# A two-layer convolution kernel on one core: the upper half of x by a rounding DMA, the lower half and the chain steps at other places in the strip

## The chip, the cores and the metric

The kernel runs on one core of one Trainium2 chip. The metric is the device time of one execution in microseconds (us). The kernel before takes 3897.72 us, the median of three runs (3897.64 to 3898.21).

## The reference

The input x is 16 images of 128 channels by 128 by 128 pixels, float32. Two layers follow, each a residual around a group normalisation (32 groups of 4 channels):

```
# layer 0
g  = group_norm(x)
xh = w_in @ g + b_in                                # 1x1, 128 -> 256 channels
k  = relu(mean(xh) @ kg_w1.T + kg_b1) @ kg_w2.T + kg_b2   # a 3x3 kernel per image and channel
y  = depthwise_conv3x3(xh, k);  y = y * tanh(softplus(y))     # Mish
x  = x + w_out @ y + b_out                          # 1x1, 256 -> 128 channels
# layer 1
f  = fftshift(fft(group_norm(x), over channels)) * mask
x  = x + relu(real(ifft(ifftshift((amp_w @ f.real + amp_b) + i*(ph_w @ f.imag + ph_b)))))
```

The transforms run over channels only, so layer 1 is one 128 by 128 matrix on the channels of each pixel, which is built once (`lt`), scaled per image by the inverse root of the variance (`lpt`), and followed by the relu.

## The kernel before, in words

An image is cut into 16 strips of 8 rows (1024 pixels, one float32 strip of 4 KB a partition). Strips are counted from 0 over all images as `n` (256 of them), and `s` is a strip's number in its image, `b` the image. Every engine runs a function `slot(n)` once a strip, with its own order of the steps written out by hand; semaphores join them. Layer 1 of strip `m = n - 19` runs in slot n.

x is used in the convolution as two float16 halves. The upper half `hi` is x rounded to float16, made by ScalarE in `cast(n + 2)` (line 371); the lower half `lo` is x minus `hi`, made by GpSimd in its `cast(n + 2)` (line 1102). Both are rings of four strips. Half of the 256 hidden channels are convolved pixel by pixel after the 1x1 product (`xh`, `side`); for these TensorE makes `product_b` (lines 681 to 683, whose result ScalarE evacuates into `xh`, line 386) and `product_side` (692 to 694). The columns from 56 on of the other half come from TensorE alone: `conv` (line 657) multiplies `hi` and `lo` by nine matrices in which the 1x1 weights and the image's 3x3 kernel are already combined, in two halves t of four rows, each in a group of five taps and a group of four. Between the groups of t = 0 stands `small_0`, between those of t = 1 `small_1`: small products of the chains below, in a bank of `psA` that `bank_0_free` and `bank_1_free` guard. `product_out` (703) is the 1x1 back to 128 channels, `layer1` (712) the matrix of layer 1.

The nine taps of the pixelwise half `accB` are shared out: three tap products on ScalarE (`tap_product`, line 413, two ahead of the evacuation of xh and one behind), two adds of these into `tsum` on GpSimd (`tap_add`, line 1110), and six multiply-adds on VectorE (`tap`, line 912), of which the first reads `tsum` in SBUF and writes `accB` in PSUM, while the others read and write `accB`. VectorE also does eight `side_tap` (924) and the residual (934). ScalarE further does the Mish activations (430, 436, 442), the squares for layer 1's statistics (462) and, for the next image, a sum and a sum of squares of each strip, which SyncE loads a second time into `XS` (450, 454). GpSimd does the two halves of the layer-1 residual (`add`, 1114). SyncE stores strip n - 20 when its adds are done and loads strip n + 3 into the same ring when that store has landed.

Once an image there are two chains. The x chain prepares the next image: group moments (TensorE, s = 10), the variance (GpSimd, end of s = 10), first guess of the inverse root (VectorE, s = 11), three Newton steps (`rstd`, end of GpSimd's s = 11), pooled products and hidden layer (s = 12), kernels and bias rows (s = 13), the nine tap matrices in three groups (`spread` on TensorE, `tap_matrices` on VectorE, `taps_halves` on GpSimd: two groups in s = 14, one in s = 15). The layer-1 chain of the image before runs in s = 1 to 3 in the same way; its `rstd` is at the end of GpSimd's s = 2 (lines 1031 to 1046) and the product `layer1_mean` that needs it in `small_0` of s = 3 (line 630). The x chain's `pooled_products` are line 593, `hidden` line 601.

In its slot GpSimd's order is: wait for VectorE's first tap of the strip, second half of the add, `cast`, chain steps, first tap add, first half of the add, second tap add, more chain steps.

Of the kernel before, what the change touches and what calls it, by code (L numbers as in the profile page):

```python
# [46 lines left out]
def conv_preact_kernel(nc, x, w_in_t, b_in, w1_t, b1, w2_t, b2, w_out_t, b_out, mask, amp_w, amp_b,  # L47
                       ph_w, ph_b, cos_m, sin_m, group_m, ident_m, valid_m, out):
    ctx = ExitStack()
    with ctx:  # L50
# [91 lines left out]
        s_hi = sem("s_hi")  # L142
# [162 lines left out]
        def _(eng):  # L305
# [55 lines left out]
            def cast(n):  # L361
                if n < STRIPS:
                    eng.wait_ge(s_first[n], 16)
                else:
                    eng.wait_ge(s_xin[n % 4], 16 * (n // 4 - 3))
                if n >= 3:
                    eng.wait_ge(s_cv, 2 * (n - 3) + 1)
                if n >= 4:
                    eng.wait_ge(s_xm, 3 * (n - 4) + 3)
                j = n % 4  # L370
                act(hi[:, 8 * j:8 * j + 8, :], rows_of(strip(n)), ACT.Copy).then_inc(s_hi, 1)  # L371

# [112 lines left out]
            cast(0)  # L485
            cast(1)
# [95 lines left out]
        def _(eng):  # L582
# [160 lines left out]
            def small_0(n):  # L743
                b, s = n // STRIPS, n % STRIPS
                if 12 <= s and b < B - 1:
                    eng.wait_ge(s_wa, 2 * n)
                    if s == 12:
                        pooled_products(b + 1, small_bank(1))
                    if s == 13:
                        kernels(b + 1, small_bank(1))  # L750
                    if s == 14:
                        spread(b + 1, 0, small_bank(1))
                    if s == 15:
                        spread(b + 1, 2, small_bank(1))
# [4 lines left out]
            def bank_1_free(n):  # L759
# [5 lines left out]
                if b < B - 1:  # L765
                    if s == 12:
                        eng.wait_ge(s_psb, b + 2)
                    if s == 13:
                        eng.wait_ge(s_ksb, b + 2)
                    if s == 14:  # L770
                        eng.wait_ge(s_wt, 3 * (b + 1) + 1)
                    if s == 15:
                        eng.wait_ge(s_wt, 3 * (b + 1) + 3)
# [3 lines left out]
            def small_1(n):  # L777
                b, s = n // STRIPS, n % STRIPS
                if b < B - 1 and s in (10, 12, 13, 14):
                    eng.wait_ge(s_wa, 2 * n + 1)  # L780
                    if s == 10:
                        group_moments("x", b + 1, small_bank(0))
                    if s == 12:
                        hidden(b + 1, small_bank(0))
                    if s == 13:
                        bias_rows(b + 1, small_bank(0))
                    if s == 14:
                        spread(b + 1, 1, small_bank(0))
# [4 lines left out]
            def bank_0_free(n):  # L793
# [4 lines left out]
                eng.wait_ge(s_wa, 2 * n - 1)  # L798
                if b < B - 1:
                    if s == 11:  # L800
                        eng.wait_ge(hk["xgsb"], b + 2)
                    if s == 13:
                        eng.wait_ge(s_hcx, b + 2)
                    if s == 14:
                        eng.wait_ge(s_vst, b + 2)
# [59 lines left out]
        def _(eng):  # L865
# [93 lines left out]
            def slot(n):  # L959
# [5 lines left out]
                if s == 11 and build:  # L965
# [4 lines left out]
                if s == 11 and build:  # L970
# [5 lines left out]
                if s == 14 and build:  # L976
                    tap_matrices(b + 1, 0, small_bank(1))
                if s == 15 and build:
                    tap_matrices(b + 1, 2, small_bank(1))
# [6 lines left out]
                if s == 14 and build:  # L986
                    tap_matrices(b + 1, 1, small_bank(0))
# [22 lines left out]
        def _(eng):  # L1010
# [87 lines left out]

            def cast(n):
                j = n % 4  # L1100
                eng.wait_ge(s_hi, n + 1)
# [17 lines left out]
            cast(0)  # L1119
            cast(1)  # L1120
# [13 lines left out]
            def slot(n):  # L1134
                b, s, m = n // STRIPS, n % STRIPS, n - LAG1

# [3 lines left out]
                if n + 2 < N:  # L1140
                    cast(n + 2)
                build = b < B - 1
# [15 lines left out]
                if s == 11 and build:  # L1158
                    rstd("x", b + 1, s_px)
                    fold(b + 1)  # L1160
                if s == 12 and build:
                    hidden_low(b + 1)
                    weights_halves(b + 1)
                if s == 14 and build:
                    taps_halves(b + 1, 1)
# [82 lines left out]
```

## Time and profile before

| what | value |
|---|---|
| profiled execution | 3897.35 us, span 3895.3 us |
| TensorE (PE) busy | 3759.3 us, 97%, granted clock 0.995 |
| VectorE (DVE) busy | 3525.0 us, 90% |
| ScalarE (ACT) busy | 3448.4 us, 89% |
| GpSimd (POOL) busy | 2632.5 us, 68% |
| DMA | 401.86 MB, 29.5% of the engines' time |
| chain that ended last | PE 77%, ACT 7%, POOL 4%, issue 3%, DVE 2% |

Times of the trace count from the start of the span. A matmul's bar includes its way through the array, so bars of neighbours overlap; what counts is the distance of their starts. The strips shown below are of the middle of the span (image 7 and the first of image 8). In this picture strip 11 of the image starts on TensorE at 1882.0, strip 12 at 1896.2, strip 13 at 1912.3, and strip 3 of the next image at 2003.2.

### The profile page before, as it was taken

What the parts mean: (1) busy time and instruction counts of PE and PEld (TensorE: products, weight loads), DVE (VectorE), ACT (ScalarE), POOL (GpSimd) and SP (SyncE); (2) the same over time, 40 slices, a digit from 0 to 9 for tenths busy, and PEclk for the clock granted to TensorE, in tenths of its full rate; (3) what the DMA queues carried; (4) which work ended last, traced back from release to release, by engine and by line L of the source; (5) the groups of instructions that cost most, each with busy time, mean ns of one, the idle gap of its engine ahead of it and who ended that gap; (6) DMA issues with size and microseconds to landing.
All of it is one profiled execution on the core that took longest, in us unless ns stands there. A gap on an engine that the chain in (4) does not pass through costs nothing.

```text
span 3895.3 us, 65845 instructions
## 1 busy us (share of the span) xinstructions
PE 3759.3 (97%) x22348; PEld 2259.9 (58%) x22348; DVE 3525.0 (90%) x4778; ACT 3448.4 (89%) x5604; POOL 2632.5 (68%) x2132
## 2 busy tenths in 40 slices
PE   4899999999999999999999999999999999999998
PEld 2555655656555555555556555565655556556554
DVE  5899989899998989989899898998989899899996
ACT  4988999898998989989899998999989999898875
POOL 3456676776767767677777767767677776777763
PEclk8999999999999999999999999999999999999999
DMA  3112333333233333333333332333333233231223
GB/s 139 64 46 85 109 108 110 103 109 114 98 114 103 109 109 105 113 104 109 103 112 111 104 110 102 112 111 103 109 104 113 105 109 111 103 113 71 74 73 124
DMA packets 111292, 401.86 MB, mean 103 GB/s; under 512 B 13232, under 2 KB 14320, under 8 KB 110704
## 3 DMA queue, kind: packets, MB, share of 16 engines
q1 hardware_dynamic: 110960, 397.66, 29.5%
q8 instruction: 181, 2.97, 0.3%
q14 instruction: 151, 1.24, 0.1%
HBM read 263.39 MB, written 134.22 MB: 102 GB/s over the span
## 4 chain that ended last, share of the span: by engine, by line
PE 77%; ACT 7%; POOL 4%; issue 3%; DVE 2%; ACTq 0%; POOLq 0%
PE psA L657 35%; PE psBO L703 19%; PE psL L712 9%; PE psBO L681 2%; PE psBO L683 2%; PE psBO L682 2%; ACT tprod L413 2%; POOL tsum L1110 2%; PE psBO L692 1%; ACT XS L454 1%; PE psBO L694 1%; PE psBO L693 1%; ACT xh L386 1%; PE psA L666 1%; DVE accS L924 1%
## 5 line engine op out<-in xcount | busy, mean ns | idle before, releaser
L657 PE MATMUL psA<-hi,wa 128*128 128x288 f16 (+4 forms) x9792 | 1938.6, 280 | 0.8 <-DVE wtmp L881 0.8
L912 DVE SCALAR_TENSOR_TENSOR accB<-xh,vectors,accB 128x1024 f32<-128x1024 f32 x1280 | 1640.1, 1281 | 0.0
L1110 POOL TENSOR_TENSOR tsum<-tsum,tprod 128x1024 f32<-128x1024 f32 x512 | 1210.6, 2364 | 315.9 <-ACT tprod L413 315.9
L924 DVE SCALAR_TENSOR_TENSOR accS<-side,vectors,accS 128x448 f32<-128x448 f32 x2048 | 1398.6, 683 | 24.1 <-ACT accS L422 14.9
L657 PE MATMUL psA<-lo,wa 128*128 128x288 f16 (+5 forms) x4896 | 1322.0, 280 | 0.0
L657 PEld LDWEIGHTS psA<-hi,wa 128*128 128x128 f16 x9792 | 926.8, 98 | 328.7 <-issue 63.0
L703 PE MATMUL psBO<-wm,woutt 128*128 128x512 f32 x2048 | 963.2, 593 | 3.6 <-DVE X L934 2.1
L1114 POOL TENSOR_TENSOR X<-X,zt 128x512 f32<-128x512 f32 x480 | 612.4, 1276 | 464.3 <-DVE accB L912 394.7
L1102 POOL TENSOR_TENSOR lo<-X,hi 128x1024 f16<-128x1024 f32 x256 | 547.6, 2139 | 359.2 <-ACT hi L371 356.9
L703 PEld LDWEIGHTS psBO<-wm,woutt 128*128 128x128 f32 x2048 | 386.5, 190 | 482.4 <-issue 481.0
L413 ACT ACTIVATE tprod<-xh,vectors 128x1024 f32<-128x1024 f32 x512 | 583.6, 1140 | 31.4 <-POOL tsum L1110 29.4
L657 PEld LDWEIGHTS psA<-lo,wa 128*128 128x128 f16 x4896 | 470.0, 98 | 222.9 <-issue 85.4
L934 DVE SCALAR_TENSOR_TENSOR X<-psBO,vectors,X 128x512 f32<-128x512 f32 x512 | 382.4, 747 | 174.1 <-PE psBO L703 174.1
L712 PE MATMUL psL<-X,lpt 128*128 128x512 f32 x960 | 490.5, 592 | 2.3 <-ACT zt L471 2.3
L912 DVE SCALAR_TENSOR_TENSOR accB<-xh,vectors,tsum 128x1024 f32<-128x1024 f32 x256 | 335.2, 1309 | 95.9 <-ACT wm L442 84.0
L386 ACT ACTIVATE xh<-psBO,vectors 128x512 f32<-128x512 f32 x510 | 348.9, 684 | 51.2 <-PE psBO L683 42.2
L471 ACT ACTIVATE zt<-psL,vectors 128x512 f32<-128x512 f32 x480 | 326.9, 681 | 37.2 <-PE psL L712 33.9
L413 ACT ACTIVATE tsum<-xh,vectors 128x1024 f32<-128x1024 f32 x256 | 291.0, 1137 | 2.9 <-DVE accB L912 2.4
L442 ACT ACTIVATE wm<-accB 128x1024 f32<-128x1024 f32 x256 | 261.1, 1020 | 16.5 <-DVE accB L912 16.5
L371 ACT ACTIVATE hi<-X 128x1024 f16<-128x1024 f32 x256 | 267.4, 1045 | 0.1
L462 ACT ACTIVATE tprod<-X 128x1024 f32<-128x1024 f32 x256 | 267.1, 1043 | 0.4 <-DVE X L934 0.2
L450 ACT ACTIVATE XS<-XS 128x1024 f32<-128x1024 f32 x240 | 251.9, 1050 | 4.2 <-DMA XS<-in_x_dram 4.2
(166 smaller groups left out, 3434.6 us busy)
## 6 DMA issues: line engine op xcount, KB each, us to landing
X<-in_x_dram SPq DMA_DIRECT2D x256, 512.0 KB, 3.3
out_dram<-X SPq DMA_DIRECT2D x256, 512.0 KB, 2.6
XS<-in_x_dram SPq DMA_DIRECT2D x240, 512.0 KB, 3.3
X<-in_w_t_dram SPq DMA_DIRECT2D x2, 1152.0 KB, 17.6
w1t<-in_w_t_dram SPq DMA_DIRECT2D x1, 256.0 KB, 2.8
wint<-in_w_in_t_dram SPq DMA_DIRECT2D x1, 128.0 KB, 2.3
woutt<-in_w_out_t_dram SPq DMA_DIRECT2D x1, 128.0 KB, 2.8
wm<-in_cos_m_dram SPq DMA_DIRECT2D x1, 64.0 KB, 4.1
```

The costliest lines, as they stand in the source:

```text
L386: act(xh[:, r0:r0 + 4, 1:1 + W], ps, ACT.Identity, bias=b1).then_inc(s_xe, 1)
L413: act(rows_of(dst[:]), xh[:, 8 * j:8 * j + 8, k:k + W], ACT.Copy, scale=kk[i % 2][:, TAPS + k:TAPS + k + 1]).then_inc(done, 1)
L471: act(zt[:, t, :], psL[:], ACT.Relu, bias=lb[:, i % 2:i % 2 + 1]).then_inc(s_re, 1)
L657: last = mm(o[:, r:r + q, 0:cols], w, src[:, at:at + q, SIDE + dx - 1:SIDE + dx - 1 + cols], start=(tap == ORDER[0] and w is wh and src is ...
L703: last = mm(psO, woutt[:, h, :], wm[:, n % 2, h, t * TP:(t + 1) * TP], start=(h == 0), stop=(h == 1))
L712: mm(psL[:], lpt[:, i % 2, :], half(m, t), start=True, stop=True).then_inc(s_lm, 1)
L912: V.scalar_tensor_tensor(out=rows_of(accB[:]), in0=xh[:, 8 * j + dy:8 * j + dy + 8, dx:dx + W], scalar=kk[i % 2][:, TAPS + k:TAPS + k + 1] ...
L924: V.scalar_tensor_tensor(out=side_out(), in0=side[:, 8 * j + dy:8 * j + dy + 8, dx:dx + SIDE], scalar=kk[i % 2][:, k:k + 1], in1=side_out( ...
L934: V.scalar_tensor_tensor(out=half(n, t), in0=psO, scalar=boutp[:, 0:1], in1=half(n, t), op0=ALU.add, op1=ALU.add, accum_out=sum1[:, k:k + ...
L1102: P.tensor_tensor(lo[:, 8 * j:8 * j + 8, :], rows_of(strip(n)), hi[:, 8 * j:8 * j + 8, :], ALU.subtract).then_inc(s_lo, 1)
L1110: P.tensor_tensor(tsum[:], tsum[:], tprod[:], ALU.add).then_inc(s_ta, 1)
L1114: P.tensor_tensor(half(m, t), half(m, t), zt[:, t, :], ALU.add).then_inc(s_add, 1)
```

## The change

- A DMA issued by GpSimd (`high`) reads the strip of x from memory, rounds it to float16 on the way and writes `hi`. ScalarE's `cast` is gone. There are four semaphores, one a ring place.
- `high(n + 3)` and `cast(n + 3)` stand in GpSimd's slot n: the first behind the first tap add, the second behind the second tap add, ahead of the variance and the Newton steps. Both were two strips ahead before. Strips 0 to 2 are made ahead of the loop.
- Seven strips carry two statistics strips each (before six), so the moments come a strip earlier.
- The x chain: moments and variance s = 9, Newton steps s = 10, pooled and hidden s = 11, kernels s = 12, bias rows s = 14, one group of three matrices in each of s = 13, 14, 15.

```diff
         def stat_strips(n):
-            if n < 6:
+            if n < 7:
                 return (2 * n, 2 * n + 1)
-            return (n + 6,) if n + 6 < STATS else ()
+            return (n + 7,) if n + 7 < STATS else ()
...
@@ scalar: slot
-                if s == 10 and build:
+                if s == 9 and build:
                     moments("x", b + 1)
...
-                if s == 12 and build:
+                if s == 11 and build:
                     pooled_out(b + 1, small_bank(1))
-                if s == 13 and build:
-                    kernels_out(b + 1, small_bank(1))
+                if s == 14 and build:
+                    bias_out(b + 1, small_bank(1))
...
-                if n + 2 < N:
-                    cast(n + 2)
...
-                if s == 10 and build:
+                if s == 9 and build:
                     stats_group("x", b + 1, small_bank(0))
+                if s == 11 and build:
+                    hidden_out(b + 1, small_bank(0))
                 if s == 12 and build:
-                    hidden_out(b + 1, small_bank(0))
-                if s == 13 and build:
-                    bias_out(b + 1, small_bank(0))
+                    kernels_out(b + 1, small_bank(0))
@@ tensor: small_0, small_1 (bank_0_free and bank_1_free wait to match)
-                if 12 <= s and b < B - 1:
+                if s in (11, 14) and b < B - 1:
                     eng.wait_ge(s_wa, 2 * n)
-                    if s == 12:
+                    if s == 11:
                         pooled_products(b + 1, small_bank(1))
...
                     if s == 14:
-                        spread(b + 1, 0, small_bank(1))
...
+                        bias_rows(b + 1, small_bank(1))
...
+                    if s == 11:
+                        hidden(b + 1, small_bank(0))
                     if s == 12:
-                        hidden(b + 1, small_bank(0))
...
+                        kernels(b + 1, small_bank(0))
+                    if s >= 13:
+                        spread(b + 1, s - 13, small_bank(0))
@@ vector: slot (root_bits and root_first at s == 10, before 11)
+                if s >= 13 and build:
+                    tap_matrices(b + 1, s - 13, small_bank(0))
@@ gpsimd
+            def high(n):
+
+                b, s, j = n // STRIPS, n % STRIPS, n % 4
+                if n >= 3:
+                    eng.wait_ge(s_cv, 2 * (n - 3) + 1)
+                if n >= 4:
+                    eng.wait_ge(s_xm, 3 * (n - 4) + 3)
+                    eng.wait_ge(s_lo, n - 3)
+                eng.dma_start(hi[:, 8 * j:8 * j + 8, :].rearrange("p r c -> p (r c)"),
+                              x[b, :, s * SP:(s + 1) * SP]).then_inc(s_hi[j], 16)
+
             def cast(n):
                 j = n % 4
-                eng.wait_ge(s_hi, n + 1)
+                eng.wait_ge(s_hi[j], 16 * (n // 4 + 1))
...
@@ gpsimd: slot
                 if m >= 1:
                     add(m - 1, 1)
-                if n + 2 < N:
-                    cast(n + 2)
...
                 if s == 12 and build:
-                    pool_bias(b + 1)
+                    hidden_low(b + 1)
+                    weights_halves(b + 1)
                 if s == 13 and build:
                     kernel_bias(b + 1)
                 if s in (14, 15) and build:
-                    taps_halves(b + 1, 0 if s == 14 else 2)
+                    taps_halves(b + 1, s - 14)
                 if n + 1 < N:
                     tap_add(n + 1, 1)
+                if n + 3 < N:
+                    high(n + 3)
+                if s == 11 and build:
+                    pool_bias(b + 1)
                 if m >= 0:
                     add(m, 0)
                 if n + 1 < N:
                     for k in range(2, EXTRA + 1):
                         tap_add(n + 1, k)
+                if n + 3 < N:
+                    cast(n + 3)
+                if s == 9 and build:
+                    variance("x", b + 1, s_px)
                 if s == 10 and build:
-                    variance("x", b + 1, s_px)
-                if s == 11 and build:
                     rstd("x", b + 1, s_px)
                     fold(b + 1)
...
+                if s == 15 and build:
+                    taps_halves(b + 1, 2)
                 if s == 1 and b >= 1:
                     variance("1", b - 1, s_p1)
                 if s == 2 and b >= 1:
```

## Rows read from the trace of the kernel before

**Rows 1.** Windows, strips 11, 12, 13, 3: length, busy per engine, PEclk, DMA, GB/s
```profile
1882.00:1896.20 14.20, 14.20 (x87) 8.63 (x86) 13.54 (x20) 13.23 (x21) 11.31 (x12) 1.00 0.33 112
1896.20:1912.30 16.10, 15.56 (x99) 9.75 (x98) 13.88 (x18) 13.78 (x25) 13.62 (x20) 1.00 0.29 98
1912.30:1930.50 18.20, 16.65 (x153) 10.24 (x152) 13.52 (x18) 14.14 (x27) 10.87 (x12) 1.00 0.25 88
2003.20:2018.90 15.70, 14.91 (x89) 8.68 (x88) 13.52 (x18) 13.35 (x22) 12.20 (x16) 1.00 0.30 101
```

**Rows 2.** Timeline of TensorE: start, us, instruction, [idle before <- releaser]
```profile
1927.28 0.37 PE L692 MATMUL psBO<-hi,wb 128*128 128x456 f16 x1 [1.55 <-ACT xh L386]
```

**Rows 3.** Busy time by stretch, start-up and two strips of the first image
```profile
28.00:32.00 4.00, 0.00 (x0) 0.00 (x0) 4.00 (x8) 0.00 (x0) 0.00 (x0) 1.00 1.05 426
102.90:119.00 16.10, 14.07 (x81) 8.05 (x80) 13.35 (x19) 14.50 (x25) 6.86 (x3) 1.00 0.20 65
167.60:180.60 13.00, 10.07 (x53) 5.05 (x52) 12.96 (x17) 12.37 (x21) 6.86 (x3) 1.00 0.22 74
```

**Rows 4.** Timeline of GpSimd (POOL), strips 11, 12 and 3
```profile
1887.01 2.36 POOL L1110 TENSOR_TENSOR tsum<-tsum,tprod 128x1024 f32<-128x1024 f32 x1 [1.05 <-ACT tprod L413]
1889.33 1.27 POOL L1114 TENSOR_TENSOR X<-X,zt 128x512 f32<-128x512 f32 x1
1890.87 2.38 POOL L1110 TENSOR_TENSOR tsum<-tsum,tprod 128x1024 f32<-128x1024 f32 x1 [0.27 <-ACT tprod L413]
...
1894.58 1.28 POOL L1033 TENSOR_TENSOR vectors<-vectors 128x1 f32<-128x1 f32 x1
...
1897.94 0.19 POOL L1046 TENSOR_TENSOR vectors<-vectors 128x1 f32<-128x1 f32 x1
...
1909.99 0.67 POOL L1093 TENSOR_TENSOR wb<-wn,wb 128x256 f16<-128x256 f32 x1
...
2005.27 0.19 POOL L1046 TENSOR_TENSOR vectors<-vectors 128x1 f32<-128x1 f32 x1
```

**Rows 5.** Timeline of TensorE, strips 11, 12 and 3
```profile
1888.59 0.38 PE L683 MATMUL psBO<-hi,wb 128*128 128x512 f16 x1
...
1898.31 0.54 PE L593 MATMUL psA<-vectors,wint 128*128 128x2 f32 x4
...
1905.50 0.95 PE L601 MATMUL psA<-vectors,w1t 128*128 128x1 f32 x8
...
2005.61 0.35 PE L630 MATMUL psA<-vectors,lt 128*128 128x1 f32 x2
```

**Rows 6.** Groups by line: count, busy us, mean ns, idle before
```profile
L371 ACT ACTIVATE hi<-X 128x1024 f16<-128x1024 f32 x256 | 267.4, 1045 | 0.1
...
L1102 POOL TENSOR_TENSOR lo<-X,hi 128x1024 f16<-128x1024 f32 x256 | 547.6, 2139 | 359.2 <-ACT hi L371 356.9 <-DVE accB L912 2.4
...
L934 DVE SCALAR_TENSOR_TENSOR X<-psBO,vectors,X 128x512 f32<-128x512 f32 x512 | 382.4, 747 | 174.1 <-PE psBO L703 174.1
```

**Rows 7.** Timeline of ScalarE (ACT), strips 11 and 12
```profile
1883.65 1.04 ACT L462 ACTIVATE tprod<-X 128x1024 f32<-128x1024 f32 x1
...
1885.73 1.14 ACT L413 ACTIVATE tprod<-xh,vectors 128x1024 f32<-128x1024 f32 x1
...
1889.01 0.69 ACT L386 ACTIVATE xh<-psBO,vectors 128x512 f32<-128x512 f32 x1
...
1898.89 0.17 ACT L327 ACTIVATE vectors<-psA 128x4 f32<-128x4 f32 x1 [1.91 <-PE psA L593]
```

**Rows 8.** Timeline of SyncE's queue, start-up
```profile
9.96 8.05 SPq L276 DMA_DIRECT2D X<-in_x_dram  x14
```

**Rows 9.** Timeline of VectorE (DVE), strips 11 and 12
```profile
1894.52 1.29 DVE L912 SCALAR_TENSOR_TENSOR accB<-xh,vectors,tsum 128x1024 f32<-128x1024 f32 x1
...
1910.10 1.65 DVE L912 SCALAR_TENSOR_TENSOR accB<-xh,vectors,tsum 128x1024 f32<-128x1024 f32 x1 [1.42 <-ACT wm L442]
```

**Rows 10.** DMA issues: count, KB each, median us to landing
```profile
X<-in_x_dram SPq DMA_DIRECT2D x256, 512.0 KB, 3.3
```

More of the change, by code:

```diff
@@ L141, in conv_preact_kernel @@
         s_valid = sem("s_valid")
-        s_hi = sem("s_hi")
+        s_hi = [sem(f"s_hi{j}") for j in range(4)]
         s_lo = sem("s_lo")
@@ L359, in edge_row @@
                     act(dst, src, ACT.Identity, bias=bias)
[L361 to L371, printed above, removed]
             def evacuate(n, t, bank=None):
@@ L484, in _ @@
             eng.wait_ge(s_zero, 5)
-            cast(0)
-            cast(1)
             stats_group("x", 0, small_bank(0))
@@ L765, in bank_1_free @@
                 if b < B - 1:
-                    if s == 12:
+                    if s == 11:
                         eng.wait_ge(s_psb, b + 2)
-                    if s == 13:
-                        eng.wait_ge(s_ksb, b + 2)
                     if s == 14:
-                        eng.wait_ge(s_wt, 3 * (b + 1) + 1)
-                    if s == 15:
-                        eng.wait_ge(s_wt, 3 * (b + 1) + 3)
+                        eng.wait_ge(s_vst, b + 2)
                 if s == 3 and b >= 1:
@@ L778, in small_1 @@
                 b, s = n // STRIPS, n % STRIPS
-                if b < B - 1 and s in (10, 12, 13, 14):
+                if b < B - 1 and s in (9, 11, 12, 13, 14, 15):
                     eng.wait_ge(s_wa, 2 * n + 1)
-                    if s == 10:
+                    if s == 9:
                         group_moments("x", b + 1, small_bank(0))
+                    if s == 11:
+                        hidden(b + 1, small_bank(0))
                     if s == 12:
-                        hidden(b + 1, small_bank(0))
[L785 to L788, printed above, removed]
+                        kernels(b + 1, small_bank(0))
+                    if s >= 13:
+                        spread(b + 1, s - 13, small_bank(0))
                 if b >= 1 and s == 1:
@@ L798, in bank_0_free @@
                 eng.wait_ge(s_wa, 2 * n - 1)
+                if s == 0:
+                    eng.wait_ge(s_wt, 3 * b + 3)
                 if b < B - 1:
-                    if s == 11:
+                    if s == 10:
                         eng.wait_ge(hk["xgsb"], b + 2)
+                    if s == 12:
+                        eng.wait_ge(s_hcx, b + 2)
                     if s == 13:
-                        eng.wait_ge(s_hcx, b + 2)
+                        eng.wait_ge(s_ksb, b + 2)
                     if s == 14:
-                        eng.wait_ge(s_vst, b + 2)
+                        eng.wait_ge(s_wt, 3 * (b + 1) + 1)
                     if s == 15:
@@ L964, in slot @@
                     residual(n - 2, 1)
-                if s == 11 and build:
+                if s == 10 and build:
                     root_bits("x", b + 1)
@@ L969, in slot @@
                 side_tap(n, 1)
-                if s == 11 and build:
+                if s == 10 and build:
                     root_first("x", b + 1)
@@ L975, in slot @@
                 side_tap(n, 2)
[L976 to L979, printed above, removed]
                 tap(n, 3)
@@ L985, in slot @@
                 side_tap(n, 5)
-                if s == 14 and build:
-                    tap_matrices(b + 1, 1, small_bank(0))
+                if s >= 13 and build:
+                    tap_matrices(b + 1, s - 13, small_bank(0))
                 tap(n, 6)
@@ L1096, in fold_1 @@
                 P.tensor_scalar(lpt[:, i % 2, :], lt[:], st["1"]["r"][:, 0:1], None, ALU.mult).then_inc(s_lpt, 1)
+            def high(n):
[7 more added lines that the diff above has]
+                              x[b, :, s * SP:(s + 1) * SP]).then_inc(s_hi[j], 16)
             def cast(n):
                 j = n % 4
-                eng.wait_ge(s_hi, n + 1)
+                eng.wait_ge(s_hi[j], 16 * (n // 4 + 1))
+                if n < STRIPS:
+                    eng.wait_ge(s_first[n], 16)
+                else:
+                    eng.wait_ge(s_xin[n % 4], 16 * (n // 4 - 3))
                 P.tensor_tensor(lo[:, 8 * j:8 * j + 8, :], rows_of(strip(n)), hi[:, 8 * j:8 * j + 8, :],
@@ L1118, in _ @@
             eng.wait_ge(s_zero, 5)
-            cast(0)
-            cast(1)
+            for n in range(3):
+                high(n)
+            for n in range(3):
+                cast(n)
             variance("x", 0, s_px)
@@ L1135, in slot @@
                 b, s, m = n // STRIPS, n % STRIPS, n - LAG1
+                build = b < B - 1
                 eng.wait_ge(s_tap, NB * n + 1)
```

11 lines of the change are left out of this document (removed).

## The prediction

> **What bounds the kernel now.** I read four views in this order: busy time by stretch, the engine timelines inside the same stretches, the groups by line, and the DMA issues. An image takes sixteen strips. In the ordinary strip [rows 1] (its first line) TensorE is busy for 14.20 of 14.20 us at the full granted clock. The other engines have idle time there: VectorE 0.66, ScalarE 0.97, GpSimd 2.9. So from the second image on TensorE sets the pace, and only its idle time can be won. The other lines of [rows 1] show where that is: 16.10 - 15.56 = 0.54 us in strip 12, 18.20 - 16.65 = 1.55 in strip 13, 15.70 - 14.91 = 0.79 in strip 3. The largest wait ends with ScalarE's evacuation of xh [rows 2], which means that ScalarE is late there. That is 2.88 us an image; every image repeats the pattern. In the first image there is no layer-1 work and TensorE isn't the bound [rows 3] (its two strip lines).
>
> The x chain now fills strips 10 to 15 and will fill 9 to 15; its inverse root is done on GpSimd at the end of strip 11 for strip 12 (after the change: 10 for 11). Two waits are on the edge now. The Newton steps of the inverse root (rstd) for layer 1 end on GpSimd at 2005.27 + 0.19 = 2005.46 [rows 4], and TensorE, after five of nine taps, starts the product that needs them at 2005.61 [rows 5], having idled 0.13. For x they end at 1898.13 [rows 4] and the product starts at 1898.31 [rows 5] with no idle.
>
> **The change part by part.** The profiled execution took 3897.35 us (span 3895.3, so 2.05 outside it), 0.4 under the median of 3897.72.
>
> *ScalarE loses the upper-half cast*: 256 passes of 1.045 us [rows 6], 267 us in all. In an ordinary strip that buys nothing, since TensorE is full. In strips 3, 12 and 13 it is more than most of what ScalarE is late by. Strip 13 loses more: the copy of the kernel products moves from ScalarE's early part, where it waited for TensorE, to the late part of strip 12. The bias copy now waits early in strip 14, about as the copy of the pooled sums does (1.91 us [rows 7]), but two products more stand there on TensorE, so I count no idle. Gain if all closes: 0.79 x 15 + (0.54 + 1.55) x 14 = 11.9 + 29.3 = 41.2 us. Its ends are 0 and 41.2; I take 41.2.
>
> *The lower half moves to the end of GpSimd's strip.* The cast of 2.14 us [rows 6] stood ahead of the first tap add, where GpSimd waited for ScalarE's product anyway, so it was free. Now it stands between the second tap add and rstd. Does the second tap add come earlier, since ScalarE is relieved? No: TensorE's product ends near 1888.97 [rows 5], ScalarE's evacuation starts at 1889.01 at once, the tap product after it, and the add at 1890.87 [rows 4, 7]. That chain hangs on TensorE. So rstd ends 2.14 later, against the same place on TensorE: the root steps and their consumers each moved one strip earlier together, which changes nothing between them. Layer 1: 2005.46 + 2.14 + 0.15 (the present delay to the product) - 2005.48 = 2.27 us idle, x 15 = 34.1. For x: 1898.13 + 2.14 + 0.15 - 1898.31 = 2.11, x 14 = 29.5. Together 63.6 us. Ends: 0 (GpSimd gets 2.1 us ahead) and 63.6; I take the upper.
>
> *The rounding DMA on GpSimd's queue.* No row shows one. Call its GpSimd time d. Below: SyncE's issue of such a 128-row transfer, 8.05 / 14 = 0.58 us [rows 8]. Above: a GpSimd pass over the strip, 2.14. GpSimd's tap add takes 2.36 us where VectorE's tap takes 1.29 [rows 4, 9], 1.8 times as long, and 1.8 x 0.58 = 1.05. I take 0.9. The Trainium skill ("DMA: Bandwidth & Descriptors", Specifications) puts first-byte latency at about 1 us for a DMA from GpSimd and 0.6 for SyncE; with 1.0 the sum would come out some 15 us higher. No row here can show it. The issue waits for the first-half convolution of the same strip, which is over before the product that ends at 1888.97 [rows 5]; the issue comes at about 1888.5 to 1889.3, so no wait. Behind it are an add, the second tap add and then VectorE's first tap. The strip itself must be in X: add 1.3, store 3.3 at most, load 3.3 [rows 10], two issues of 0.6: 9.1 us after GpSimd's strip starts, and the cast comes at 11.
>
> *A loop that closes.* VectorE's first tap reads xh and tsum, both in SBUF. A GpSimd step of normally 0.19 us took 1.28 at 1894.58 beside that tap at 1894.52 [rows 4, 9], and the tap took 1.65 instead of 1.29 at 1910.10 beside a GpSimd pass begun at 1909.99: they exclude each other. The other taps accumulate in PSUM and show nothing of the kind. Today GpSimd is idle when the first tap runs. Now the cast runs there, from 1893.2 to 1895.3, and the tap waits for it. That closes a loop: residual, squares and two tap products on ScalarE 3.22 (1883.65 to 1886.87), 0.14, tap add 2.32, d, add 1.27, tap add 2.38, cast 2.14, first tap 1.29, residual 0.75 [rows 4, 6, 7, 9]: 13.4 after 0.1 of overlaps, plus d: 14.3 us against a strip of 14.2. TensorE doesn't wait for this loop in an ordinary strip, but rstd rides on it. It gains lateness of 0.1 a strip over six strips, and 0.7 is left from strip 3, where rstd's own lateness restarts the loop some 4 us late (estimate): 1.3 at rstd for x, 0.5 for layer 1, which comes after the long strips 12 to 14. 1.3 x 14 + 0.5 x 15 = 25.7 us. Ends: 0 at d = 0.58 (loop 14.0) and some 140 at d = 2.14, where the loop of 15.5 is the pace. The Trainium skill ("SBUF — State Buffer", Who interferes with whom) says that a VectorE instruction with two SBUF inputs contends with a GpSimd instruction that reads SBUF, whichever issues first blocking the other; both durations above agree. The same section speaks against GpSimd's DMAs beside VectorE's two-port modes.
>
> *A second stall in strip 11*: the pooled bias now stands behind the first tap add and the DMA. From the pooled product at 1898.31, ScalarE is free at 1899.0 [rows 5, 7]; + 3.22 + 0.14 + 2.32 + 0.9 + 0.4 for the two small steps = 1906.0, while TensorE wants it 7.19 after, at 1905.50. 0.5 x 14 = 7 us. Ends 0 and 24 (d = 2.14).
>
> *The rest.* Kernels, spreads, bias rows and tap matrices keep their instructions, one matrix a strip, each now on inputs that were made a strip or half a strip before; the rest of the strip before is what hides them: 0. Without that age one of them could cost a step like the 0.67 us pass at 1909.99 [rows 4]. First image: five strips of two statistics each, bound by ScalarE (14.50 busy of 16.1 [rows 3]), lose 1.04 each: -5.2. A sixth, now 13.0, becomes such a strip of 15.1: +2.1. Its chain strips: -3 (ends 0 and -8). Three more strips (1.57 MB) are read while the DMAs run at 426 GB/s [rows 3]: 3.7 us, of which I estimate 2.3 as slack, since VectorE's statistics are 4.00 busy of 4.00 there: +1.4. Together -4.7.
>
> Sum: 3897.35 - 41.2 + 63.6 + 25.7 + 7 - 4.7 = 3947.8; the median some 0.4 higher: **3948 us**.
>
> **Rivals.** *The relief wins* (0.20): GpSimd's phase against TensorE moves forward by over 2.1 us and the inverse roots are in time. Speaks for it: 2.9 us of idle on GpSimd, 1.0 more on ScalarE, and the first tap add does start 0.8 earlier. Against: the second add's chain above. It decides at the start of the second tap add: below 1888.8 in the strip shown there is no stall. Then 3897.35 - 41.2 - 4.7 = 3851 us.
> *Half way* (0.12): the stalls are about 1 us each, no drift: 3851 + 29 x 1.2 = 3886, up to 3905 with some second stalls.
> *The upper half lands late* (0.18): a strip's load takes 3.3 us to land [rows 10] with a third of the DMA time busy [rows 1]. Over 6 us, the first tap starts ahead of the cast, the loop opens, but the cast ends 1.29 + 1.3 = 2.5 later: + 29 x 2.5 - 25.7 = +47, 3995 us. With d at 1.5 the drift gives about as much.
> That a DMA's rounding differs from ScalarE's changes no time: the lower half is taken as the difference to what landed.
>
> **How the numbers follow.** The forecast has 0.50, its own range 3915 (d = 0.58: no drift, second stall 0.2) to 3975. The likeliest gives 3948. The range for 8 in 10 is 3870 to 3998: it takes in the half-way case and the late landing, and leaves out most of the relief's 0.20. A difference of under 0.2% (7.8 us) can't be told from none. Faster: 0.20 + 0.03 of the half-way case = 0.23; same: the rest of it = 0.09; slower: 0.68.
>
> **What would show it.** In strips 3 and 11 TensorE idles 2 to 4 us before the layer-1 mean product and before the pooled product, released by GpSimd's last rstd step; strip 11 has a second idle of 0.5 before the hidden product. The waits for xh in strips 3, 12 and 13 are gone. The first tap shows over 1.29 us or starts as the cast ends. GpSimd's DMA issue takes 0.6 to 1.2 us. Wrong if GpSimd's rstd ends before TensorE's fifth tap, or if the strips without chain steps are longer than 14.2 us.

## The result, and the profile after the change

Medians of four runs each, taken in turn on one chip: 3897.97 us before (3897.64 to 3899.13), 3950.61 us after (3941.92 to 3956.06). The ratio is 1.0132 [1.0114, 1.0151]: slower by 52.6 us, where 3948 was forecast. The total was right, and several terms of it were not: the two largest errors, a drift that didn't come (25.7 us) and a clock that was not in the sum (23.6 us), have opposite signs and nearly cancel. That is luck. The profiled execution took 3950.64 us, its span 3948.9.

Busy time by stretch, the columns of [rows 1]: strip 9, whose one chain step on TensorE is a small product, then strips 11, 12 and 13 of the same image and strip 3 of the next.

```profile
1882.00:1896.10 14.10, 14.10 (x80) 8.36 (x79) 14.06 (x19) 13.12 (x23) 10.92 (x7) 1.00 0.45 130
...
1910.20:1928.20 18.00, 15.81 (x99) 9.82 (x98) 15.39 (x19) 12.95 (x24) 14.22 (x24) 1.00 0.37 103
...
1928.20:1944.20 16.00, 16.00 (x159) 10.43 (x158) 13.83 (x19) 12.70 (x21) 11.76 (x10) 1.00 0.40 116
1944.20:1959.00 14.80, 14.80 (x84) 9.05 (x83) 13.46 (x19) 12.69 (x21) 10.54 (x12) 1.00 0.42 126
...
2031.63:2050.19 18.56, 16.21 (x89) 9.60 (x88) 15.66 (x19) 12.62 (x21) 13.87 (x22) 0.91 0.35 100
```

The reader is to see three things. A strip without waits has no TensorE idle time and is no longer than before (strips 4 to 8 take 14.15 to 14.18 us in both kernels, medians over images 2 to 13). Strips 12 and 13 have closed their gaps (16.00 of 16.00, with many small products of the kernel step, and 14.80 of 14.80). Strips 11 and 3 now hold idle time of 18.00 - 15.81 = 2.19 and 18.56 - 16.21 = 2.35 us, and in strip 3 the granted clock is down to 0.91.

What TensorE waited for (us in total, times, longest) names the cause of both:

```profile
PE psA L614 <- POOL vectors L1022: 39.3, 16, 5.5
PE psA L577 <- POOL vectors L1022: 36.3, 16, 5.5
PE psBO L676 <- ACT xh L374: 8.3, 12, 1.4
```

L614 is the layer-1 mean product of strip 3, L577 the pooled product of strip 11, L1022 the last step of the inverse root. From the second image on it is 33.8 us over 15 waits (2.25 each) and 28.9 over 14 (2.06 each). The third line is what remains of the wait of [rows 2], which in the kernel before read:

```profile
PE psBO L692 <- ACT xh L386: 45.5, 55, 2.0
```

The two waits on TensorE's timeline (start, us, instruction, idle before it), and two pairs of convolution products on either side of the second:

```profile
1914.53 0.58 PE L577 MATMUL psA<-vectors,wint 128*128 128x2 f32 x4 [2.07 <-POOL vectors L1022]
...
2032.46 0.41 PE L641 MATMUL psA<-hi,wa 128*128 128x288 f16 x2
...
2036.21 0.35 PE L614 MATMUL psA<-vectors,lt 128*128 128x1 f32 x2 [2.35 <-POOL vectors L1022]
...
2037.37 0.68 PE L641 MATMUL psA<-hi,wa 128*128 128x288 f16 x2
```

The same pair takes 0.41 us before the wait and 0.68 behind it. The stretches show why (PEclk, the granted clock, is the third column from the end). The last line is strip 3 of an earlier image, whose wait of 2.12 us was not followed by a lower clock:

```profile
2031.60:2035.80 4.20, 2.26 (x17) 1.38 (x15) 4.20 (x7) 0.80 (x2) 3.14 (x14) 1.00 0.00 0
2036.70:2040.10 3.40, 3.40 (x14) 2.08 (x12) 3.40 (x4) 3.40 (x6) 1.40 (x2) 0.50 0.33 137
...
831.46:848.20 16.74, 14.62 (x90) 8.77 (x89) 13.95 (x19) 12.55 (x21) 12.08 (x22) 1.00 0.36 108
```

From 0.5 us behind the end of the wait TensorE was granted its lower level, 1.2 instead of 2.4 GHz, for 3.4 us. Between 200 and 3850 us of the span this happened nowhere before and in 13 places after, 51 us together. Each begins between 0.5 us ahead of the end of one of the two waits and 1.1 us behind it: 12 at strip 3's (of 15) and one at strip 11's (of 14). Over the whole span the time at the lower level went from 38.4 to 92.9 us.

What such a stretch costs can be read inside this one execution. Without its idle time strip 3 takes 14.62 us in the three images that keep the full clock and 16.22 (median) in the eleven with 3.4 us at the lower level, so 1.60 us each. The twelfth has 6.8 us of it and takes 17.66, and the one strip 11 with 6.8 us takes 18.90 where the others take 15.94. Together 11 x 1.60 + 3.04 + 2.96 = 23.6 us.

GpSimd's timeline through strip 10 and into strip 11 answers to [rows 4]:

```profile
1900.44 2.37 POOL L1101 TENSOR_TENSOR tsum<-tsum,tprod 128x1024 f32<-128x1024 f32 x1 [2.42 <-ACT tprod L401]
1902.74 0.62 POOL L1083 DMA_DIRECT2D hi<-in_x_dram  x1
...
1905.17 2.37 POOL L1101 TENSOR_TENSOR tsum<-tsum,tprod 128x1024 f32<-128x1024 f32 x1 [0.50 <-issue]
1907.49 2.14 POOL L1093 TENSOR_TENSOR lo<-X,hi 128x1024 f16<-128x1024 f32 x1
1909.58 1.18 POOL L1007 TENSOR_TENSOR vectors<-vectors 128x1 f32<-128x1 f32 x1
...
1914.20 0.19 POOL L1022 TENSOR_TENSOR vectors<-vectors 128x1 f32<-128x1 f32 x1
```

The first tap add still waits 2.42 us for ScalarE's product. The cast stands behind the second add, the Newton steps start when it ends, and the last of them ends at 1914.39, 0.14 before TensorE starts L577. VectorE's first tap in the same strip:

```profile
1908.57 2.15 DVE L892 SCALAR_TENSOR_TENSOR accB<-xh,vectors,tsum 128x1024 f32<-128x1024 f32 x1
```

It begins 1.08 us into the cast and takes 2.15 us, where [rows 9] has 1.29 (the mean before is 1.309). The small step at 1909.58 in turn takes 1.18 us beside the tap. By lines (count, busy us, mean ns) and DMA issues (KB, median us to landing):

```profile
L892 DVE SCALAR_TENSOR_TENSOR accB<-xh,vectors,tsum 128x1024 f32<-128x1024 f32 x256 | 497.3, 1943 | 97.9 <-ACT wm L430 50.2
...
L1093 POOL TENSOR_TENSOR lo<-X,hi 128x1024 f16<-128x1024 f32 x256 | 548.6, 2143 | 17.2 <-DMA hi<-in_x_dram 14.8
...
hi<-in_x_dram POOLq DMA_DIRECT2D x256, 256.0 KB, 3.6
```

GpSimd's time at an issue of that DMA has a median of 0.577 us over the 256 (0.547 to 0.732). The rounded strip lands 3.6 us later (3.4 to 12.1), and the cast waits for it 14.8 us in the whole kernel: the DMA is cheap and in time.

### The profile page after: what moved, and what is told of

Same layout as the page of the kernel before. It is cut to its first block and busy times, and to the rows that moved or that the text cites. A ratio compares the mean times of both kernels' runs of the same rounds, so it can differ in the third digit from the quotient of the medians.

```text
span 3948.9 us, 66039 instructions
## 1 busy us (share of the span) xinstructions
PE 3785.6 (96%) x22348; PEld 2273.9 (58%) x22348; DVE 3679.2 (93%) x4778; ACT 3248.7 (82%) x5348; POOL 2797.9 (71%) x2388
## 3 DMA queue, kind: packets, MB, share of 16 engines
q1 hardware_dynamic: 110960, 397.66, 28.9%
## 5 line engine op out<-in xcount | busy, mean ns | idle before, releaser
L892 DVE SCALAR_TENSOR_TENSOR accB<-xh,vectors,tsum 128x1024 f32<-128x1024 f32 x256 | 497.3, 1943 | 97.9 <-ACT wm L430 50.2
L1093 POOL TENSOR_TENSOR lo<-X,hi 128x1024 f16<-128x1024 f32 x256 | 548.6, 2143 | 17.2 <-DMA hi<-in_x_dram 14.8
L430 ACT ACTIVATE wm<-accB 128x1024 f32<-128x1024 f32 x256 | 261.3, 1021 | 40.2 <-DVE accB L892 39.9
L438 ACT ACTIVATE XS<-XS 128x1024 f32<-128x1024 f32 x240 | 251.5, 1048 | 5.8 <-DMA XS<-in_x_dram 5.7
L442 ACT ACTIVATE XS<-XS 128x1024 f32<-128x1024 f32 x240 | 250.9, 1045 | 0.2
```

Source lines behind the costliest of these rows:

```text
L892: V.scalar_tensor_tensor(out=rows_of(accB[:]), in0=xh[:, 8 * j + dy:8 * j + dy + 8, dx:dx + W], scalar=kk[i % 2][:, TAPS + k:TAPS + k + 1] ...
L1093: P.tensor_tensor(lo[:, 8 * j:8 * j + 8, :], rows_of(strip(n)), hi[:, 8 * j:8 * j + 8, :], ALU.subtract).then_inc(s_lo, 1)
```

## The experiments

The theory: in the two strips with a chain, the cast of 2.14 us now stands between the second tap add and the inverse root, and TensorE waits for that. Everything else (the DMA, the matrices one a strip, the chain a strip earlier) costs nothing or pays. The rivals: it is the DMA on GpSimd's queue; it is the earlier chain; the loop through first tap and cast sets the pace. Each run stood beside the kernel before on the same chip (medians 3895.6 to 3900.2 us); the ratio is to that. Differences in us between two kernels below are of their medians, and those of different chips can be off by the 4.6 us that the kernel before moved by. After the first, each kernel of an experiment ran four times.

**Chain ahead of the cast** (after, changed): in strips 1, 2, 9 and 10 the variance and Newton steps stand ahead of the cast.

```diff
-                if n + 3 < N:
-                    cast(n + 3)
                 ... (variance, Newton steps)
+                if n + 3 < N:
+                    cast(n + 3)
```

> The changed kernel, but GpSimd's variance and Newton steps stand ahead of the lower-half cast in strips 1, 2, 9 and 10 instead of behind it. Theory (the chain stands behind a 2.14 us cast, and TensorE waits 2.25 us in strip 3 and 2.06 in strip 11, after which its clock falls to half for 3.4 us in many images): both waits go below 0.3 us, the half-clock time falls from 95 us to about 41 as in the kernel before, and the time is 3951 - 34 - 29 - 27 = 3861 us, range 3850 to 3880. Rival (the DMA on GpSimd's queue, or VectorE's first tap held up by the cast, 1943 against 1309 ns, costs the time): both are still there in every strip, so 3930 to 3951.

3889.19 us (3885.88 to 3891.54, seven runs), ratio 0.997 [0.996, 0.998]. TensorE's wait and VectorE's first tap:

```profile
PE psA L614 <- POOL vectors L1022: 12.3, 14, 5.5
...
L892 DVE SCALAR_TENSOR_TENSOR accB<-xh,vectors,tsum 128x1024 f32<-128x1024 f32 x256 | 471.3, 1841 | 40.9 <-POOL tsum L1101 29.6 <-ACT wm L430 11.2
```

With the cast out of the chain's way in 4 of 16 strips the loss of 52 us turns into a gain of 11. The sign is as expected, the size 28 us short and outside the expected range. The layer-1 wait is still 0.53 us in most images, and the side product of strip 1 waits 0.5 to 0.8 us for ScalarE in 8 of 14. The cast now reaches into the next strip; in the one shown VectorE's first tap begins 0.07 us behind the start of the cast and takes 3.14 us:

```profile
1986.44 2.12 POOL L1093 TENSOR_TENSOR lo<-X,hi 128x1024 f16<-128x1024 f32 x1
...
1986.51 3.14 DVE L892 SCALAR_TENSOR_TENSOR accB<-xh,vectors,tsum 128x1024 f32<-128x1024 f32 x1
```

On average the first tap is nearly as long as in the kernel after (1.84 against 1.94), without the loss.

**The DMA alone** (before, changed): the rounding DMA behind the first tap add, cast(n + 2) in its old place, the chain and the matrices as before.

```diff
-                if n + 2 < N:
-                    cast(n + 2)          (ScalarE's upper half)
+                if n + 3 < N:
+                    high(n + 3)          (GpSimd, behind the first tap add)
```

> The kernel before with one part of the change: the upper half by the rounding DMA, issued three strips ahead behind the first tap add; the lower half (two strips ahead, ahead of the first tap add), the statistics and all chain steps stay where they were before. Theory: nothing new stands ahead of the Newton steps but 0.58 us of issue, hidden by the wait for ScalarE; the waits for xh close (41 us an execution) and the start-up costs 4: 3898 - 41 + 4 = 3861, range 3850 to 3885. Rival (the DMA costs the time, by GpSimd's time, by traffic or by the port): 3930 or more.

3854.32 us (3852.75 to 3855.34), ratio 0.988 [0.987, 0.990], 7 us below the expected and inside its range. TensorE's waits for the inverse roots are those of the first image alone; the start costs 22.2 us where it cost 18.4:

```profile
PE psA L572 <- DVE vectors L857: 22.2, 1, 22.2
...
PE psA L577 <- POOL vectors L1030: 5.5, 1, 5.5
PE psA L614 <- POOL vectors L1030: 5.5, 1, 5.5
...
L896 DVE SCALAR_TENSOR_TENSOR accB<-xh,vectors,tsum 128x1024 f32<-128x1024 f32 x256 | 331.4, 1295 | 56.0 <-ACT wm L430 40.0 <-POOL tsum L1109 15.9
```

An image takes 233.2 us instead of 236.2. The DMA on GpSimd's queue isn't the loss; it is the gain.

**The order without the DMA** (after, changed): ScalarE makes the upper half of strip n + 3 at the place of its strip that corresponds.

```diff
+            def upper(n):                (ScalarE)
+                ...
+                act(hi[:, 8 * j:8 * j + 8, :], rows_of(strip(n)), ACT.Copy).then_inc(s_hi, 1)
-                if n + 3 < N:
-                    high(n + 3)
```

> The changed kernel with the upper half made by ScalarE again (three strips ahead, behind the last tap product) and no DMA on GpSimd; all of the order stays changed. Theory: the waits of 2.2 us in strips 3 and 11 stay, and ScalarE's 1.05 us a strip comes back on top: 3950 to 3990 us. Rival (the DMA costs the time): about 3898 or less.

4047.35 us (4043.74 to 4048.79), ratio 1.038 [1.036, 1.039]: over 57 us above the expected range.

```profile
PE psBO L693 <- ACT xh L387: 122.6, 181, 3.4
PE psA L631 <- POOL vectors L1039: 29.0, 16, 5.5
PE psA L594 <- POOL vectors L1039: 28.7, 16, 5.4
...
L909 DVE SCALAR_TENSOR_TENSOR accB<-xh,vectors,tsum 128x1024 f32<-128x1024 f32 x256 | 438.2, 1712 | 137.9 <-ACT wm L443 124.9 <-POOL tsum L1107 7.6
```

ScalarE is late for the side product in most strips (181 waits). Its pass of 1.05 us now stands ahead of the second evacuation of xh, which the side product waits for; that buries the size. Two things still read clearly. Both inverse-root waits are there with no DMA (1.5 us in most images), and so is the long first tap: they come with the cast's place.

**Products that fill the waits** (after, changed): 16 products of 128x288 whose result nobody reads, ahead of each of the two waiting products.

```diff
+            def filler(b):
+                for q in range(16):
+                    mm(psA[:, 1, 128:128 + 288], wa[:, b % 2, 0, 0:C],
+                       wa[:, b % 2, 0, C:C + 288], start=True, stop=True)
                     if s == 11:
+                        filler(b)
                         pooled_products(b + 1, small_bank(1))
                 if s == 3 and b >= 1:
+                    filler(b)
                     layer1_mean(b - 1, small_bank(1))
```

> The changed kernel with 16 added products (128x288 float16, about 2.0 us) whose result nobody reads, ahead of the product in strip 11 and of the one in strip 3 that wait for the Newton steps, so that TensorE works where it idled. The output is computed in full. Theory (the idle time drops the clock, which costs some 27 us beside the 63 of the waits themselves): the steps after the waits start when they did, the clock stays at full as in the kernel before, and the time falls to 3951 - 27 = 3924, range 3918 to 3932. Rival (the half-clock intervals have another cause or cost nothing): 3946 to 3956.

3935.01 us (3934.31 to 3938.91), ratio 1.009 [1.008, 1.010]: 15.6 us less than the kernel after, though TensorE has more to do, and 3 us above the expected range. Strip 11 by stretch, and the wait that is left:

```profile
1903.50:1921.50 18.00, 17.83 (x116) 11.39 (x115) 13.93 (x19) 13.00 (x24) 14.33 (x24) 1.00 0.37 103
```

```profile
PE psA L614 <- POOL vectors L1029: 10.9, 10, 5.5
```

The strip is as long as without the filling (18.0), so the chain sets its end whatever TensorE does. At neither of the two waits is there a stretch at the lower level any more, instead of 51 us. So the idle time is what brought the lower clock, and the fill gave back some 15.6 us (the four runs after spread over 14 us, so this is rough). It is less than the 23.6 us read above because the fill adds a little of its own: it takes 16 x 0.12 = 1.9 us, and some waits were hardly longer. From the other side, half the work at half the clock puts a ceiling of (92.9 - 38.4) / 2 = 27 us on the cost.

**Two issues for one** (after, changed): each rounding DMA in two halves, so that GpSimd pays 2 x 0.573 = 1.15 us a strip.

```diff
-                eng.dma_start(hi[:, 8 * j:8 * j + 8, :]...,
-                              x[b, :, s * SP:(s + 1) * SP]).then_inc(s_hi[j], 16)
+                for t in range(2):
+                    eng.dma_start(hi[:, 8 * j + 4 * t:8 * j + 4 * t + 4, :]...,
+                                  x[b, :, s * SP + t * TP:s * SP + (t + 1) * TP]).then_inc(s_hi[j], 16)
```

> The changed kernel with each upper-half DMA split into two of four rows, so that GpSimd spends some 1.16 us a strip on issues instead of 0.58; bytes and all else alike. The prediction's loop (13.4 us plus the issue time) is then 14.56 us against strips of 14.2 on average. Theory of the prediction (lateness gathers from strip to strip and rstd rides on it): the two waits of TensorE grow to some 5.0 us in strip 11 and 4.2 in strip 3, and the time goes to about 4020 us, range 4000 to 4040. Rival (the loop has slack that the prediction overlooked; the drift doesn't exist): only the second wait in strip 11 grows, by 0.5 us, so 3957, range 3945 to 3970.

4007.75 us (4005.35 to 4017.93), ratio 1.029 [1.028, 1.031].

```profile
PE psA L614 <- POOL vectors L1022: 51.4, 16, 5.5
PE psA L577 <- POOL vectors L1022: 47.5, 16, 5.5
```

The time is inside the expected range, but the waits are not what was expected: they rise by 0.8 us each, to (51.4 - 5.5) / 15 = 3.06 us in strip 3 and to 2.87 in strip 11 (from the second image on), where 4.2 and 5.0 were named. The time at the lower clock is up as well, from 92.9 to 127.0 us. The forecast's loop is at work here, but more weakly than it had it. The second tap add starts 9.04 us after TensorE's strip in strip 4, then 9.14, 9.29, 9.49, 9.60, 9.70 and 9.82 in strips 5 to 10 (medians over images 2 to 13): 0.13 a strip. In the kernel after it stays between 8.84 and 9.1 in all of them. These strips are 14.19 us long on average, so the loop takes some 14.32 us with d = 1.15 (d is the forecast's name for GpSimd's time at the issue), and some 13.2 without it (an estimate: 14.32 - 1.15).

**The start mended** (the DMA alone, changed): ScalarE makes the upper halves of strips 0 and 1, and the DMA of strip 2 is issued behind the folded weights, so that the first read of x is alone.

```diff
+            for n in range(2):           (ScalarE)
+                eng.wait_ge(s_first[n], 16)
+                act(hi[:, 8 * n:8 * n + 8, :], rows_of(strip(n)), ACT.Copy).then_inc(s_hf, 1)
-            for n in range(3):           (GpSimd, at its start)
-                high(n)
+            high(2)                      (GpSimd, behind the folded weights)
```

> The kernel of e2 (the DMA alone), but the upper halves of strips 0 and 1 come from ScalarE as in the kernel before, and the DMA for strip 2 is issued after the folded weights are made, when the start-up loads are over. Theory (the 3.9 us that the first convolution comes later, 68.1 against 64.2, are the 1.57 MB read among the start-up loads): the first convolution starts at about 64.3 and the time is 3854 - 4 = 3850. Rival (the delay is GpSimd's, from issuing and casting ahead of the first variance): 3854.

3845.65 us (3843.76 to 3845.90), ratio 0.987 [0.985, 0.988], 4 us below the expected. It beats both kernels and is the fastest version found. The start's wait is back at the 18.4 us of the kernel before:

```profile
PE psA L576 <- DVE vectors L861: 18.3, 1, 18.3
```

**The cast back in front** (after, changed): all of the change but the cast's place. Ahead of the loop two casts stand instead of three.

```diff
             (GpSimd's strip, ahead of the first tap add)
+                if n + 2 < N:
+                    cast(n + 2)
             (at its end)
-                if n + 3 < N:
-                    cast(n + 3)
```

> The changed kernel with one part undone: the lower half again two strips ahead and ahead of the first tap add; DMA, statistics and chain steps as in the change. It splits the 35 us that the kernel with the chain first (3889) is above the kernel with the DMA alone (3854). Theory (the cast at the strip's end costs, since VectorE's first tap waits for it, 1.84 against 1.30 us, and the first tap add of strips 3 and 11 comes late): 3854, range 3848 to 3862, first tap at 1.30 us. Rival (moving the statistics and chain steps a strip earlier costs it): 3885 or more.

3858.06 us (3857.64 to 3858.83), ratio 0.990 [0.989, 0.992]. The end of the chain in a strip 3 and the next cast on GpSimd, and TensorE's product:

```profile
1984.98 0.19 POOL L1022 TENSOR_TENSOR vectors<-vectors 128x1 f32<-128x1 f32 x1
...
1987.16 2.15 POOL L1093 TENSOR_TENSOR lo<-X,hi 128x1024 f16<-128x1024 f32 x1
```

```profile
1985.32 0.35 PE L614 MATMUL psA<-vectors,lt 128*128 128x1 f32 x2
```

No idle time stands ahead of the product, and it starts 0.15 after the root: on the edge, as [rows 4, 5] had it. The move of the cast costs 3950.61 - 3858.06 = 92.6 us, more than the whole loss. What the earlier chain and the matrices one a strip cost is the small rest against the DMA alone, 3858.06 - 3854.32 = 3.7 us, which is within the spread between chips. In the two profiled executions 2.5 us of it lie in the first image and 1.7 in the next 14, whose length is 233.2 us in both kernels, although the hidden product of strip 11 now waits 0.31 us:

```profile
PE psA L585 <- POOL vectors L1036: 6.1, 16, 1.0
```

**Two casts of sixteen** (the kernel just above, changed): the cast at the strip's end, ahead of the Newton steps, in strips 2 and 10 only. These two hold two casts, strips 3 and 11 none.

```diff
-                if n + 2 < N:
+                if n + 2 < N and s not in (3, 11):
                     cast(n + 2)
                 ...
+                if s in (2, 10) and n + 3 < N:
+                    cast(n + 3)
```

> The kernel of e7 (DMA and chain steps as in the change, lower half in front and two ahead), except that in strips 2 and 10, the two with the Newton steps, the lower half of strip n + 3 is also made ahead of them, as in the change, and strips 3 and 11 make none. Two casts in sixteen stand where the change puts all. Theory (only the casts ahead of the Newton steps cost): the waits of 2.2 and 2.1 us are back, 15 x 2.2 + 14 x 2.1 = 62, with the clock's 16 to 27 on top: 3858 + 78 to 89 = 3936 to 3947 us. Rival (the cast at the end of the ordinary strips carries part of the loss): well under 3930, and the more so the larger its part.

3944.83 us (3942.15 to 3946.45), ratio 1.013 [1.011, 1.014]. GpSimd's cast and root, TensorE's product, and the first tap:

```profile
2023.34 2.13 POOL L1093 TENSOR_TENSOR lo<-X,hi 128x1024 f16<-128x1024 f32 x1
...
2030.07 0.19 POOL L1022 TENSOR_TENSOR vectors<-vectors 128x1 f32<-128x1 f32 x1
```

```profile
2030.40 0.44 PE L614 MATMUL psA<-vectors,lt 128*128 128x1 f32 x2 [2.08 <-POOL vectors L1022]
```

```profile
L892 DVE SCALAR_TENSOR_TENSOR accB<-xh,vectors,tsum 128x1024 f32<-128x1024 f32 x256 | 356.0, 1391 | 99.7 <-ACT wm L430 51.2 <-POOL tsum L1101 48.4
```

Two casts of sixteen make 3944.83 - 3858.06 = 86.8 of the 92.6 us. The first tap is near its old length (mean 1.391 instead of 1.943, with 30 of 256 above 1.5), and that gives back only the last 6, no more than the spread between chips. So the loop of cast and first tap through every strip costs next to nothing, and the one pass in front of the Newton steps nearly everything. The lower clock is part of that price: it follows 13 of the 15 waits of strip 3 here, and strip 3 without its idle time again takes 16.2 us with it and 14.6 without.

## Why the prediction was right, and where it was not

| term of the sum | forecast | measured |
|---|---|---|
| waits for xh closed | -41.2 | 3.0 us an image over 14 images, -42 (the DMA alone) |
| inverse roots late | 2.27 x 15 + 2.11 x 14 = 63.6 | 33.8 + 28.9 = 62.7 |
| drift of the loop | +25.7 | 0 |
| second wait, strip 11 | +7 | 0.12 x 13 = 1.5 |
| start and first image | -4.7 | +4.0 - 0.9 = +3.1 |
| TensorE's clock | not in it | +23.6 |
| sum | +50.4 | +48.9; the medians differ by 52.6 |

The 3.7 us that are left are near what strips 3 and 11 have grown by beyond idle time and clock: against the kernel with the cast in front they are 0.09 and 0.27 us longer, 5.1 us in 15 and 14 of them, of which 1.5 is the second wait.

*The relief of ScalarE* held, place and size. The kernel with the cast in front has it together with the changed start, 3858.06 - 3897.97 = -39.9 (-39.0 against its own kernel before), against the forecast's -41.2 - 4.7 = -45.9; the start and first image account for most of the difference.

*The two waits* held to 1 us in 63, and the two strips with the cast alone in its new place show that they are the cast's. The argument that carried it was that the second tap add hangs on TensorE's own product and not on ScalarE's load. The rival that the relief wins was to decide there: "below 1888.8 in the strip shown there is no stall". The corresponding add after comes at 1890.62, some 8.9 us into a strip, no earlier than before.

*The GpSimd time of the issue, d,* was the mis-sized term. I took 0.9, scaling SyncE's issue by a ratio of two elementwise passes. The measured 0.577 is the lower bound that the forecast had named, SyncE's 8.05 / 14 = 0.575 [rows 8]: an issue is no pass over data, and the ratio of passes said nothing of it. The Trainium skill ("DMA: Bandwidth & Descriptors", Specifications) has about 1 us to the first byte for GpSimd against 0.6 for SyncE; the issue on the engine shows nothing of that difference. At the landing there is at most a trace of it, 3.6 against 3.3 us [rows 10], with another size and a conversion in it.

*The drift* failed with d. The forecast's own figure for d = 0.58 was a loop of 14.0 under the strip of 14.2 and no drift, and that is what the kernel did. With twice the issue the drift came, 0.13 a strip, where the forecast's loop of 13.4 + 1.15 = 14.55 would gain some 0.35. So the mechanism exists, beyond a point that this change doesn't reach, and its base is some 13.2 us and not the 13.4 that I had added up.

*The lock between first tap and cast* held as a fact (1.31 to 1.94 us on average, 201 of 256 taps above 1.5; also without the DMA, and not with the cast in front) and failed as a cost. It is the rule of the Trainium skill ("SBUF — State Buffer", Who interferes with whom) that the forecast weighed; the trace agrees, with a tap of 2.15 us begun 1.08 into a cast of 2.14. The strips without a chain are as long as before with it, so nobody waits for VectorE there.

*The start.* Three more strips of x are read while all the DMA time is in use. I estimated 2.3 of the 3.7 us as slack, on the ground that VectorE's statistics were the busier. There was none: the first convolution starts at 68.2 instead of 64.2 us, and with the first read mended it was at 64.0 again. The stretch that I had looked at, 28 to 32 us [rows 3], is not the one that decides. VectorE loses its time earlier, between 16 and 26 us, in four waits for x that sum to 4.0 us, where before it had one of 0.8. The same stretch after and before:

```profile
20.00:24.00 4.00, 0.00 (x0) 0.00 (x0) 1.78 (x3) 0.00 (x0) 2.94 (x2) 1.00 1.08 304
20.00:24.00 4.00, 0.00 (x0) 0.00 (x0) 4.00 (x7) 0.00 (x0) 2.12 (x2) 1.00 1.03 420
```

The strips of the first image gave back only 0.9 us instead of the 6.1 that I had counted; 1.1 us of the difference is its own wait for the inverse root, 1.89 us where it was 0.78.

*What I had not seen* is the clock: waits of over 2 us in a stream that from the second image on had almost none of that length. With d right, my sum would have been the 3915 that the forecast gives for that case (it drops the second wait there, too; the 0.2 us that the text keeps would make it 3918), and the kernel took 3951. The clock (23.6) and the start and first image (7.8 above the forecast) fill 31 of these 36 us. So the forecast's mechanism and its price are confirmed, and its total owes part of its closeness to an error of one sign beside an omission of the other.

What stays open: why the chain ahead of the cast stays 31 us above the cast in front. In the traces 2.0 us an image of it lie in strips 1, 2, 3 and 11 (0.64, 0.39, 0.68 and 0.29 us longer, medians), where its cast stands beside the next strip's first tap or small waits are left; no run took these one by one. Open too is why the lower clock comes at strip 3's wait and hardly at strip 11's, which is as long.

## What to carry to other kernels

Before moving a pass to an engine's "idle end of the strip", look for what stands behind it there: the engine had nearly 3 us of idle time a strip, and a pass of 2.14 us cost 3 us in each of the two strips of an image where a chain on the edge followed. Test a bundle of edits by parts: here one part gave 3854.32 - 3900.23 = -46 us by itself, another costs some 92, the rest about nothing, and the bundle was kept from a gain of 1.0% by the place of one pass in two strips of sixteen. Price an instruction of a new kind by the nearest instruction of that kind, on whatever engine, not by a ratio of unlike ones, and price a new wait of microseconds on a full TensorE at more than its length (here 62.7 us of waits brought 23.6 us of lower clock).

## What the hardware showed that I had not expected

- A wait of some 2.2 us on a TensorE that was otherwise full went with 3.4 us, twice 6.8 us, at the 1.2 GHz level in 13 of 29 cases, with waits of 1.9 to 2.7 us, and nearly always at the wait of strip 3, though that of strip 11 is as long. A stretch of 3.4 us cost 1.60 us. With products that nobody reads in the wait, none was left there, and the kernel took 15.6 us less.
- A DMA that rounds 256 KB of fp16 out of fp32 costs GpSimd 0.577 us, and halving it leaves the cost of each issue at 0.573. It lands after 3.6 us with 36 to 45% of the DMA time in use in the strips shown (3.8 to 3.9 in the other kernels with one issue a strip), and it has no visible effect on VectorE: with it and the cast in front the first tap takes 1.289 to 1.295 us on average.
- The lock works both ways at once: a tap begun 1.08 us into a cast takes 2.15 us, and a small GpSimd step of normally 0.19 us, queued behind the cast, takes 1.18 beside that tap.
